# A projection with its split operands stacked by DMA, and 125-row loads in two pieces

## What is computed

```python
e = jnp.stack([tbl_0[ids[:, 0]], ..., tbl_38[ids[:, 38]]], axis=1)   # (2048, 39, 64)
delta = jnp.einsum('uf,bfe->bue', inner_w, e)                        # inner_w (128, 39)
z = jnp.sum(delta * delta, axis=-1)                                  # (2048, 128)
h = jnp.concatenate([z, dense_ctx], axis=1)                          # (2048, 144)
h = jnp.maximum(h @ W_top1 + b_top1, 0.0)                            # (2048, 512)
h = jnp.maximum(h @ W_top2 + b_top2, 0.0)                            # (2048, 256)
y = h @ W_top3
```

## Time and profile before

| | us |
|---|---|
| median of 3 runs (lowest, highest) | 608.44 (608.41, 608.72) |
| span of the profiled execution | 701.7 |
| TensorE busy | 639.5 (91%) |
| VectorE busy | 436.0 (62%) |
| GpSimd busy | 420.6 (60%) |
| ScalarE busy | 257.2 (37%) |

### The profile page before, as it was taken

How to read it: one execution, slowest core, us unless ns; L and a number is a source line. 1 busy time by engine, 2 the same in 40 slices (tenths; PEclk the granted TensorE clock), 3 DMA queues, 4 the chain that set the end, 5 groups by cost and what they waited for, 6 DMA issues and landing times.

```text
span 701.7 us, 10994 instructions
## 1 busy us (share of the span) xinstructions
PE 639.5 (91%) x4000; PEld 579.0 (83%) x4000; DVE 436.0 (62%) x821; ACT 257.2 (37%) x314; POOL 420.6 (60%) x407
## 2 busy tenths in 40 slices
PE   0045899999999999989999999989999999999998
PEld 0044799999979998889989998889988999899994
DVE  3159768766756765657655676657755677456560
ACT  1146243334324343324334242234424333244542
POOL 6777377777773777457771777647772677700000
PEclk9985666666666666666666666666666666666666
DMA  5544554135111611033111621134110521100000
GB/s 78 115 132 129 121 77 88 24 47 97 37 25 38 102 31 26 19 77 68 26 25 23 93 45 25 25 61 79 25 26 16 89 52 25 24 3 1 2 1 0
DMA packets 34790, 34.99 MB, mean 50 GB/s; under 512 B 10047, under 2 KB 26434, under 8 KB 34728
## 3 DMA queue, kind: packets, MB, share of 16 engines
q0 software_dynamic: 12800, 13.13, 15.6%
q1 hardware_dynamic: 21928, 21.18, 10.9%
q10 hardware_dynamic: 16, 0.01, 0.0%
HBM read 34.28 MB, written 0.01 MB: 49 GB/s over the span
## 4 chain that ended last, share of the span: by engine, by line
PE 87%; SPq 5%; DVE 4%; DMA 2%; ACT 1%; issue 1%
PE side L343 29%; PE delta L403 12%; PE delta L405 12%; PE delta L404 12%; PE turned L387 10%; PE side L367 6%; SPq L260 4%; PE side L359 3%; DMA x_all<-tbl 2%; PE side L372 2%; DVE onehot L560 1%; PE side L360 1%; DVE table L631 1%; DVE x_all L628 1%; DVE x_all L573 0%
## 5 line engine op out<-in xcount | busy, mean ns | idle before, releaser
L301 POOL DMA_INDIRECT x_all<-tbl,idx x400 | 419.8, 1050 | 192.3 <-issue 119.8
L343 PE MATMUL side<-table,onehot 125*128 125x192 bf16 x1856 | 242.5, 309 | 53.8 <-DVE table L631 42.7
L343 PEld LDWEIGHTS side<-table,onehot 125*128 125x128 bf16 x1856 | 202.7, 122 | 82.5 <-issue 44.9
L581 DVE TENSOR_TENSOR acc_all<-acc_all,sq 128x1024 f32<-128x1024 f32 x120 | 147.1, 1226 | 116.4 <-ACT sq L476 116.1
L476 ACT ACTIVATE sq<-delta 128x1024 f32<-128x1024 f32 x120 | 123.0, 1025 | 214.8 <-PE delta L405 214.4
L403 PE MATMUL delta<-xh,wjh 117*128 117x256 f32 x512 | 183.3, 358 | 3.8 <-issue 3.8
L405 PE MATMUL delta<-xh,wjl 117*128 117x256 f32 x512 | 176.0, 344 | 0.0
L404 PE MATMUL delta<-xl,wjh 117*128 117x256 f32 x512 | 175.5, 343 | 0.0
L560 DVE TENSOR_SCALAR onehot<-idh,row_no 125x512 bf16<-125x512 f16 x464 | 141.3, 375 | 10.6 <-ACT idh L455 10.4
L403 PEld LDWEIGHTS delta<-xh,wjh 117*128 117x128 f32 x512 | 125.0, 244 | 10.3 <-issue 8.3
L405 PEld LDWEIGHTS delta<-xh,wjl 117*128 117x128 f32 x512 | 128.4, 251 | 0.0
(11 more groups left out here) (36 smaller groups left out, 141.9 us busy)
## 6 DMA issues: line engine op xcount, KB each, us to landing
idb<-ids_by_field SPq DMA_DIRECT2D x9, 1250.0 KB
x_all<-tbl,idx POOLq DMA_INDIRECT x400, 3.2
idb<-ids_by_field SPq DMA_DIRECT2D x9, 500.0 KB
x_all<-tbl SPq DMA_DIRECT2D x12, 250.0 KB
x_all<-tbl SPq DMA_DIRECT2D x2, 312.5 KB
w2s<-W_top SPq DMA_DIRECT2D x1, 512.0 KB, 7.0
idx<-ids SPq DMA_DIRECT2D x16, 19.5 KB, 1.8
w1z<-W_top SPq DMA_DIRECT2D x1, 256.0 KB, 19.4
```

The source lines that it names most:

```text
L301: pool.indirect_dma_start(x_slots[k][:, f, 0:E], None, tables[f], bass.IndirectOffsetOnAxis(idx[k][:, f:f + 1], 0),).then_inc(gathered[k], 16)
L343: mm = pe.matmul(side[n % 2][:, q * PARTS * E:(q + 1) * PARTS * E], onehot[k % OHR][:, c, q, h * TB:(h + 1) * TB], table[k][:, q, c, :, :] ...
L581: dve.tensor_tensor(acc[p][:, :], acc[p][:, :], sq[(quad - 1) % SQ][:, :], ALU.add).then_inc(summed, 1)
```

## The change

- **Stacking.** After the high and the low half of a unit are made, SP copies them by DMA within SBUF into a tile `xs` of 117 rows: rows 0 to 38 high, 39 to 77 low, 78 to 116 high again, for each of the 3 copies j a block of 512 columns (`restack`: nine DMAs for each unit, each 39 rows of 2 KB, source every third partition). The weights `ws` are stacked alike: high, high, low. One matmul of 512 columns then gives what six gave: 2 columns e, all three products. `xs` has three buffers (XS).
- **Waits.** The projection waits for the landed copies (`stacked`) in place of `xl_ready`; the high half of a later unit waits for the copies that read its buffer in place of the projection; `restack` waits for the projection of three units before.
- **Timetable.** The transposes come up to 5.2 groups ahead of the projection, the first ones 3.6 ahead of the step. SQ and OHR go from 3 to 2.
- **Loads.** Each load of 125 rows (ids and tables) is two DMAs, of 112 and of 13 rows.
- **SP's loop** is written out; the loads of idx and idb for step s + 2 come after the second unit of step s.
- The weights are loaded to adjacent partitions, and split by one subtraction and three copies.

```diff
-ORDER = [(g // 2, g % 2, j) for g in range(EG) for j in range(J) if g + EG * j < E]
-QUADS = len(ORDER) // 4
-FIRST_OF_UNIT = [min(n for n, o in enumerate(ORDER) if o[0] == u) for u in range(UNITS)] + [E]
+ORDER = [(u, j) for u in range(UNITS) for j in range(J) if 2 * u + 1 + EG * j < E]
+QUADS = len(ORDER) // 2
+FIRST_OF_UNIT = [min(n for n, o in enumerate(ORDER) if o[0] == u) for u in range(UNITS)] + [E // 2]
 XR = 4
-SQ = 3
-OHR = 3
+XS = 3
+MOVES = 3 * J
+SQ = 2
+OHR = 2
...
+LEAD = 5.2
 START = -4
-TURN_AT = [-1.2, -1.2] + [2 * u - 4.3 for u in range(2, UNITS)]
+WIDE = (slice(0, 112), slice(112, KP))
+TURN_AT = [max(2 * u - LEAD, 0.3 * u - 3.6) for u in range(UNITS)]
...
-QUAD_AT = [2 * ORDER[4 * q + 3][0] + ORDER[4 * q + 3][1] for q in range(QUADS)]
+PAIR_AT = [2 * u + 0.6 * j for u, j in ORDER]
+QUAD_AT = [PAIR_AT[2 * q + 1] + 0.6 for q in range(QUADS)]
...
-        wj = [sb(f"wj{j}", [KT, U], F32) for j in range(J)]
-        wjh = [sb(f"wjh{j}", [KT, U], F32R) for j in range(J)]
-        wjl = [sb(f"wjl{j}", [KT, U], F32R) for j in range(J)]
+        xs = [sb(f"xs{k}", [3 * F, J, 2, NB], F32R) for k in range(XS)]
+        w3t = sb("w3t", [3 * F, U], F32)
+        wh3 = sb("wh3", [3 * F, U], F32R)
+        ws = sb("ws", [3 * F, U], F32R)
...
+        def at_stack(s, u):
+            uses = len(range(u % XS, UNITS, XS))
+            return (s * uses + u // XS + 1) * (16 * MOVES)
...
-                        sp.dma_start(idb[:, fields, :], src.partition_broadcast(KP)).then_inc(idb_in[half], 16)
+                        for rows in WIDE:
+                            sp.dma_start(idb[rows, fields, :], src.partition_broadcast(rows.stop - rows.start)).then_inc(idb_in[half], 16)
...
-                        sp.dma_start(stage[k][:, q, :, :], tables[2 * k + q].rearrange("(p c) e -> p c e", c=ch)).then_inc(tables_in[k], 16)
+                        for rows in WIDE:
+                            sp.dma_start(stage[k][rows, q, :, :], tables[2 * k + q].rearrange("(p c) e -> p c e", c=ch)[rows, :, :]).then_inc(tables_in[k], 16)
...
-                        sp.wait_ge(wj_zero, J)
-                        for j in range(J):
-                            sp.dma_start(wj[j][j:KT:J, :], w_t).then_inc(wj_in, 16)
+                        for c in range(3):
+                            sp.dma_start(w3t[c * F:(c + 1) * F, :], w_t).then_inc(wj_in, 16)
...
+                def restack(s, u):
+                    if u >= XS or not (isinstance(s, int) and s == 0):
+                        last = u - XS if u >= XS else last_in_ring(UNITS, XS, u % XS)
+                        sp.wait_ge(projected, at_quads(s if u >= XS else s - 1) + (FIRST_OF_UNIT[last + 1] - 1) // 2 + 1)
+                    to = xs[u % XS]
+                    for ready, half, copies in ((xh_ready, xh, (0, 2)), (xl_ready, xl, (1,))):
+                        sp.wait_ge(ready, at_units(s) + u + 1)
+                        for c in copies:
+                            for j in range(J):
+                                sp.dma_start(to[c * F:(c + 1) * F, j, :, :].bitcast(F32),
+                                             half[j:KT:J, u % XR, :, :].bitcast(F32)).then_inc(stacked[u % XS], 16)
+
                 def step(s, p):
-                    for k in (2 * p, 2 * p + 1):
-                        sp.wait_ge(gathered[k], (s - p) * (8 * (F - N_ONEHOT)))
-                        load_idx(s, k)
-                    sp.wait_ge(cast, s * 2)
-                    load_idb(s)
...
+                    for u in range(UNITS):
+                        restack(s, u)
+                        if u == 1 and s < STEPS - 2:
+                            for k in (2 * p, 2 * p + 1):
+                                sp.wait_ge(gathered[k], (s - p + 2) * (8 * (F - N_ONEHOT)))
+                                load_idx(s + 2, k)
+                        if u == 1 and s < STEPS - 1:
+                            sp.wait_ge(cast, s * 2 + 4)
+                            load_idb(min(s + 2, STEPS - 1))
...
-                def project(s, group):
-                    u, g = group // 2, group % 2
-                    if g == 0:
-                        pe.wait_ge(xl_ready, at_units(s) + u + 1)
...
-                        pe.matmul(o, wjh[j][:, :], xh[:, u % XR, g, :], start=True, stop=False)
-                        pe.matmul(o, wjh[j][:, :], xl[:, u % XR, g, :], start=False, stop=False)
-                        mm = pe.matmul(o, wjl[j][:, :], xh[:, u % XR, g, :], start=False, stop=True)
...
+                def project(s, n):
+                    u, j = ORDER[n]
+                    if j == 0:
+                        pe.wait_ge(stacked[u % XS], at_stack(s, u))
+                    quad = n // 2
+                    if n % 2 == 0:
+                        wait(pe, squared, at_quads(s) + quad - 1)
+                    mm = pe.matmul(delta[quad % 2][:, (n % 2) * 2 * NB:(n % 2 + 1) * 2 * NB], ws[:, :],
+                                   xs[u % XS][:, j, :, :].rearrange("p g b -> p (g b)"), start=True, stop=True)
+                    if n % 2 == 1:
+                        mm.then_inc(projected, 1)
...
                 def free_xr(s, u):
+                    if isinstance(s, int) and s == 0 and u < XR:
+                        return
                     last = u - XR if u >= XR else last_in_ring(UNITS, XR, u % XR)
-                    wait(act, projected, at_quads(s if u >= XR else s - 1) + (FIRST_OF_UNIT[last + 1] - 1) // 4 + 1)
+                    act.wait_ge(stacked[last % XS], at_stack(s if u >= XR else s - 1, last))
```

More of the change, by code:

```diff
@@ L205, in build @@
         dense_low = sem("dense_low")
-        wj_high = sem("wj_high")
-        wj_low = sem("wj_low")
+        stacked = [sem(f"stacked{k}") for k in range(XS)]
+        w_high = sem("w_high")
+        w_low = sem("w_low")
+        w_ready = sem("w_ready")
         projected = sem("projected")
@@ L276, in _ @@
                     sp.dma_start(b2s[:, :], b2.rearrange("(k p) -> p k", p=P)).then_inc(stored[1], 16)
-                def step(s, p):
-                    for k in (2 * p, 2 * p + 1):
-                        sp.wait_ge(gathered[k], (s - p) * (8 * (F - N_ONEHOT)))
-                        load_idx(s, k)
-                    sp.wait_ge(cast, s * 2)
-                    load_idb(s)
-                supersteps(sp, step, 2, STEPS - 1)
-                sp.wait_ge(cast, STEPS * 2)
-                load_idb(STEPS - 1)
+                def restack(s, u):
[9 more added lines that the diff above has]
+                                             half[j:KT:J, u % XR, :, :].bitcast(F32)).then_inc(stacked[u % XS], 16)
+                def step(s, p):
+                    for u in range(UNITS):
[7 more added lines that the diff above has]
+                            load_idb(min(s + 2, STEPS - 1))
+                for s in range(STEPS):
+                    step(s, s % 2)
                 for k in range(2):
@@ L389, in transpose @@
                     mm.then_inc(turned_up, 1)
-                def project(s, group):
-                    u, g = group // 2, group % 2
-                    if g == 0:
-                        pe.wait_ge(xl_ready, at_units(s) + u + 1)
-                    for n in range(len(ORDER)):
-                        if ORDER[n][:2] != (u, g):
-                            continue
-                        j = ORDER[n][2]
-                        quad = n // 4
-                        if n % 4 == 0:
-                            wait(pe, squared, at_quads(s) + quad - 1)
-                        o = delta[quad % 2][:, (n % 4) * NB:(n % 4 + 1) * NB]
-                        pe.matmul(o, wjh[j][:, :], xh[:, u % XR, g, :], start=True, stop=False)
-                        pe.matmul(o, wjh[j][:, :], xl[:, u % XR, g, :], start=False, stop=False)
-                        mm = pe.matmul(o, wjl[j][:, :], xh[:, u % XR, g, :], start=False, stop=True)
-                        if n % 4 == 3:
-                            mm.then_inc(projected, 1)
+                def project(s, n):
[9 more added lines that the diff above has]
+                        mm.then_inc(projected, 1)
                 def rows(s):
@@ L412, in rows @@
                         todo += [(TURN_AT[u] + TURN_LAG, "transpose", u) for u in range(UNITS)]
-                        todo += [(g, "project", g) for g in range(EG)]
+                        todo += [(PAIR_AT[n], "project", n) for n in range(len(ORDER))]
                     if in_range(s, last=STEPS - 2):
@@ L451, in cast_ids @@
                     fields = HALVES[half]
-                    act.wait_ge(idb_in[half], s * 16 + 16)
+                    act.wait_ge(idb_in[half], (s + 1) * (16 * len(WIDE)))
                     if half == 0:
@@ L524, in _ @@
                     if k == STAGES - 1:
-                        act.wait_ge(wj_in, 16 * J)
-                        for j in range(J):
-                            act.activation(wjh[j][:, :], wj[j][:, :], ACT.Copy).then_inc(wj_high, 1)
+                        act.wait_ge(wj_in, 16 * 3)
```

(11 more changed lines are left out.)

9 lines of the change are left out of this document (4 added, 5 removed).

## The result

| | before | after |
|---|---|---|
| median of 4 runs, us (lowest, highest) | 608.42 (608.16, 608.72) | 850.66 (850.01, 851.25) |
| ratio, 95% interval | 1 | 1.3994 (1.3967 to 1.402) |
| span of the profiled execution | 701.7 | 849.4 |
| TensorE busy | 639.5 | 435.6 |

The change makes the kernel 40% slower: it takes 242 us more. TensorE is busy 204 us less, but only a part of that is work saved, since the two profiles differ in the granted clock (0.67 on average before, 0.75 after).

A forecast was written before the change was run, and what follows sets the result against it. Gathers bind the timed steps, TensorE the tail. Gathers from 70.2 plus 7 x 67.4, landing, SP's last 99 copies and the end give 608.6 us profiled; less 3.5 for TensorE's clock, about 605; range 552 to 632.

The forecast's parts named there:

- The bound of the timed kernel before: Timed runs: GpSimd's gathers bind the steps at 67.4 us each, TensorE the tail, at a clock of about 0.81.
- The projection on TensorE: Steps: TensorE falls from 80.4 to 59.7 us a step at 0.65; none of it shows in the timed steps.
- The split loads: Start: GpSimd's second row of gathers begins at 70.2 instead of 80.81 us, gaining 10.6; bounds 0 and 10.6.
- Rival 4: Start: loading 125 rows in two pieces brings nothing, 615.6 us; chance 5%.
- The cost of one issue: SP's stacking copies: 0.38 us each with gap, 37.6 us a step, under 67.4; bound reached at 0.65 each.
- The bytes: Stacking copies: 719 KB a unit at 296 GB/s, 2.4 us a unit, 27 a step; only the landing charged.
- rival 5: Steps: the copies' bytes bind at 84 GB/s, 8.6 us a unit, 855 us in all; chance 3%.
- rival 1: Steps: SP is the new bound, 792 issues at 0.79 us are 626 us, 742 in all; chance 17%.
- The waits: Projection, waiting for landed copies: 16 us of lead cover 1.6 (transposes, high half), 3.4 of issue, 2.2 of landing.
- The fewer buffers: Squares and one-hots: two fewer buffers cost VectorE and ScalarE waits of a group or less, in slack: nothing.

The follow-up runs named there:

- six copies: The changed kernel without the second copy of the high half, so six stacking copies a unit instead of nine, all from SP: 724.26 us, ratio 1.1916.
- two issuers: The changed kernel with ScalarE issuing the three copies of the low half and SP the six of the high half: 764.45 us, ratio 1.2593.

## Why the prediction was wrong

**The bound of the timed kernel before: right.** Gathers in the steps, TensorE at the end, as worked out from the earlier trace rows. Less TensorE brings little, fewer gathers bring much. The clock was higher than the 0.81 I took: 0.93 to 0.94 in the runs of the kernel before on other chips. I had chosen 0.81 because the sum then meets 608; at 0.94 it gives 602 us, and some 6 us stay unexplained. The 0.65 of the earlier trace rows belongs to that one execution.

**The projection on TensorE: right, and worth nothing.** TensorE fell to 435.6 us and then stood. (Not from 639.5, which was at a clock of 0.65: the fair figure is the 492.5 of the split loads at 0.94.)

**The split loads: right in sign, 6.9 us of at most 10.6.** I had the first tables by 15 to 25 us; the ten-field broadcast ahead of them kept them to 32.60. The "Don't bother" of the Trainium skill (DMA: Bandwidth & Descriptors, "Rules for kernel authors") is said of two halves that each go over all 16 DMA engines, and doesn't carry over to a row count of 125: alone the split brings 1.1%, in the changed kernel 41 us. Rival 4 is out.

**The cost of one issue: the step that failed.** I took 0.38 us with its gap; it is 0.79. I had two kinds of rows: those from HBM to adjacent partitions or a broadcast (0.27 to 0.41) and the weight copies (0.744). I called the second kind the nearest in form, and then went by the first, because full queues seemed to explain the difference. The single issues show that they explain nothing: 0.750 for that weight copy and 0.743 for the copy within SBUF, both with empty queues. That an issue within SBUF costs twice one from HBM no row of before could show; that the explanation by full queues was a guess, and that SP would be the bound above 0.65 us, the text itself said. The choice deserved even chances, not 17%. The estimate of 0.43 us by the Trainium skill's 512 cycles (DMA: Bandwidth & Descriptors, "Why a DMA increments its semaphore by 16 and not by 1") is too low as well: 0.743 was measured.

**The bytes: right.** 2.4 us a unit and hidden; a quarter of them changes 0.5%. 102 GB/s at a share of 0.33 [the stretch of the profile after] is 309 GB/s for all engines busy, against the 296 I took. So the 855 us of rival 5 lie 4 us from the result by chance and not by its mechanism.

**From rival 1's 742 us to 850.66.** The mechanism and the 0.79 us are rival 1's; its sum lacked 109 us. On SP's timeline (176 groups of copies) the copies take 702.9 us instead of the 615.1 of 88 x (4.68 + 2.31): 88 us of standing, nearly all behind the seven broadcasts. Rival 1 had left that out, and so had the whole prediction: it said of the broadcasts only that they are needed a step later and so covered, and not what they do to the copies behind them. The idx and idb issues take 27.4 us, not 18 (+9). The first copy starts at 83.1, not 74.7 (+8): the last gather before it landed after 11.6 us, and 3.2 had been taken. Waits between the groups are about 7, the end is 4 or 5 shorter, and 1.3 lie around the span. Together 742 + 88 + 9 + 8 + 7 - 4.5 + 1.3 = 851.

**The waits: no cover at that price.** I let 16 us of lead cover 7 us of round. With SP behind by a whole stretch of units no lead helps. And the landing that I put at 2.2 us is 2.2 only away from the broadcasts. Right behind one it was 10.3 to 11.5 us in the changed kernel and 13.6 to 15.3 where SP had room (six copies, two issuers), and there it took back some 82 us and more of what was forecast. The range, 552 to 632, left out rivals 1 and 5; with rival 1 in it, it would have reached 742 and still missed.

**The fewer buffers: nothing, as said.** No run changes them alone. In the profile after, ScalarE waited 2.2 us for a buffer of squares and VectorE 9.6 us for TensorE at the one-hots.

Left open: why an issue with SBUF on both sides costs twice one from HBM; why SP stands behind a broadcast for so long and why the copies then land so late, for which the only run with a small broadcast was a disturbed one; and what an order of SP's issues that keeps the copies away from the broadcast would give.

## What to carry to other kernels

Count the issues of every small DMA that a change adds, multiply by the price of the same form (SBUF or HBM source, strided or adjacent destination) measured alone, and compare the sum with the step, before looking at bytes. When two rows of the trace give prices that are a factor of two apart on either side of the point from which the new engine binds, the one nearest in form decides until something shows otherwise. A large broadcast among many small copies costs twice, in their issue and in their landing, and another engine's queue doesn't escape it (5.98 us for three copies on ScalarE's). A load of 125 rows should be cut into 112 and 13.

## What the runs showed of the hardware

- An issue on SP's queue, nothing else running: 0.743 us for 39 rows within SBUF whatever stride and bytes, 0.759 for 117 rows, 0.590 for 32 and 0.608 for 112; 0.370 for 39 rows from HBM to adjacent partitions, 0.750 to every third one; 0.786 within SBUF on ScalarE's queue. By the Trainium skill (DMA: Bandwidth & Descriptors, "Why a DMA increments its semaphore by 16 and not by 1") 39 and 117 rows are spread over 13 DMA engines, 32 and 112 over 16. The prices within SBUF group in this way; those from HBM don't (0.421 for 32 rows, 0.370 for 39).
- Behind 1.75 MB of a broadcast in pieces of 1 KB SP stood some 12 us a step, and 20.1 us in one issue when the broadcast wasn't split. The copies right behind it landed after 10.3 to 15.3 us instead of 2.2.
- A gather's issue takes 0.95 us in most places, and 1.62 and 1.65 in the two shown beside a VectorE sum of two SBUF operands; with one operand in PSUM, none beside a sum takes more than 0.95, and the mean of all falls from 1.044 to 0.959.
- The same kernel was profiled at a granted clock of 0.65 (span 701.7) and ran at 0.93 to 0.944 in its later runs of 605 to 610 us.
